# A recommendation tower on one core: the last tiles multiplied without rounding, two items fetched ahead of the second tile's rows

## What is computed

```
e = stack([tbl_f[ids[:, f]] for f in 0..25], axis=1)
z = concat([dense, all products of pairs of (dense, e)])
h = concat([z, dense])
h = maximum(h @ W_top1 + b_top1, 0)      # 607 -> 512
h = maximum(h @ W_top2 + b_top2, 0)      # 512 -> 256
y = h @ W_top3                           # 256 -> 1
```

## Time and profile before

| what | us |
|---|---|
| median of 3 runs | 472.18 (470.95 to 473.91) |
| the profiled execution: its time | 471.37 |
| the profiled execution: its span, first to last instruction | 469.5 |
| POOL busy / PE busy / DVE busy / ACT busy | 396.2 / 417.1 / 338.4 / 223.7 |
| mean granted TensorE clock | 0.967 |

### The profile page before, as it was taken

One profiled execution on the slowest core, in us unless ns is written; L12 is line 12 of the kernel. 1 busy time (PEld: TensorE's weight loads), 2 busy tenths in 40 slices (PEclk: granted clock), 3 DMA queues, 4 the chain that ended last, 5 costly groups with the idle time before them and its releaser, 6 DMA issues.

```text
span 469.5 us, 11728 instructions
## 1 busy us (share of the span) xinstructions
PE 417.1 (89%) x4210; PEld 392.8 (84%) x4210; DVE 338.4 (72%) x777; ACT 223.7 (48%) x727; POOL 396.2 (84%) x553
## 2 busy tenths in 40 slices
PE   0766969989999989998799969999699988999898
PEld 0766869889999979898798969999698978988786
DVE  5897897986888677885597657876678855956260
ACT  3853654536553535455254443545254552536152
POOL 7899999899989998998998998899899899899600
PEclk9988997999999989999899999999899998999999
DMA  7992225122212312231212312222122212121100
GB/s 213 263 227 83 78 80 168 51 75 77 78 44 79 83 39 86 74 82 43 80 45 74 87 40 80 51 77 74 45 82 74 83 43 80 41 80 41 35 2 0
DMA packets 20046, 36.82 MB, mean 78 GB/s; under 512 B 8109, under 2 KB 10677, under 8 KB 19994
## 3 DMA queue, kind: packets, MB, share of 16 engines
q0 software_dynamic: 8704, 17.84, 14.3%
q1 hardware_dynamic: 11290, 18.28, 13.7%
HBM read 36.09 MB, written 0.01 MB: 77 GB/s over the span
## 4 chain that ended last, share of the span: by engine, by line
POOL 55%; issue 28%; PE 6%; DMA 3%; ACT 3%; DVE 2%; SPq 1%; POOLq 1%; DVEq 0%; ACTq 0%
POOL rows L414 29%; POOL y_wide L403 25%; DMA vecs<-in_tbl 3%; PE turn_ps L489 2%; PE dots_ps L473 1%; DVE inter L889 1%; POOLq L402 1%; ACT dots_ps L686 1%; SPq L297 1%; PE turn_ps L554 1%; PE mlp_ps L563 1%; DVE onehot L836 1%; ACT t_hi L679 1%; PE dots_ps L554 1%; DVE t_lo L853 1%
## 5 line engine op out<-in xcount | busy, mean ns | idle before, releaser
L414 POOL DMA_INDIRECT rows<-in_tbl,idx_sb x272 | 261.9, 963 | 45.6 <-POOL y_wide L403 43.7
L836 DVE TENSOR_TENSOR onehot<-ids_sb,late_ps 125x1024 fp32r<-125x1024 int32 (+2 forms) x154 | 167.3, 1143 | 8.2 <-DMA ids_sb<-in_ids_by_round 4.5
L889 DVE COPY_PREDICATED inter<-mask,dots_ps 27x48 f32<-27x48 int32 x496 | 103.1, 208 | 63.0 <-ACT inter L703 44.2
L403 POOL MEMSET y_wide<- 64x448 f32 x272 | 134.2, 493 | 0.2
L703 ACT COPY inter<-dots_ps 27x64 f32<-27x64 f32 x496 | 99.4, 200 | 67.0 <-PE dots_ps L473 54.5
L473 PE MATMUL dots_ps<-vecs 128*64 128x54 f32 x1984 | 117.3, 224 | 1.5 <-ACT vecs L672 0.9
L473 PEld LDWEIGHTS dots_ps<-vecs 128*64 128x64 f32 x1984 | 113.3, 139 | 5.8 <-issue 2.1
L489 PE MATMUL turn_ps<-onehot,t_hi 125*128 125x256 f32 x378 | 103.6, 309 | 13.6 <-DVE vecs L652 10.3
L489 PE MATMUL turn_ps<-onehot,t_lo 125*128 125x256 f32 x378 | 98.3, 295 | 0.0
L489 PEld LDWEIGHTS turn_ps<-onehot,t_hi 125*128 125x128 f32 x378 | 77.5, 205 | 18.5 <-issue 8.5
L489 PEld LDWEIGHTS turn_ps<-onehot,t_lo 125*128 125x128 f32 x378 | 77.5, 205 | 0.2
(11 more groups left out here) (86 smaller groups left out, 371.8 us busy)
## 6 DMA issues: line engine op xcount, KB each, us to landing
ids_sb<-in_ids_by_round SPq DMA_DIRECT2D x25, 384.0 KB
rows<-in_tbl,idx_sb POOLq DMA_INDIRECT x272
vecs<-in_tbl SPq DMA_DIRECT2D x8, 448.0 KB
rows<-in_r_dense_features SPq DMA_DIRECT2D x16, 64.0 KB
h_sb<-in_W_top_laid SPq DMA_DIRECT2D x2, 512.0 KB
vecs<-in_tbl SPq DMA_DIRECT2D x1, 560.0 KB
w_sb<-in_W_top SPq DMA_DIRECT2D x1, 512.0 KB
vecs<-in_tbl SPq DMA_DIRECT2D x8, 52.0 KB
```

The lines of the kernel that those rows point to most:

```text
L403: pool.memset(unread, 0.0).then_inc(pauses_made, 1)
L414: nc.gpsimd.indirect_dma_start(out=rows[v % 2][:, s, :], out_offset=None, in_=tables[f - 1][:, :], in_offset=bass.IndirectOffsetOnAxis(ap= ...
L836: dve.tensor_tensor(part_buffer(k, h)[0:KP, 0:n], home.rearrange("p (o r) -> p o r", o=1).to_broadcast([KP, n, R]), row_of[KT[k]][0:KP, a: ...
L889: dve.copy_predicated(inter_of(u, q, g, a, n), mask[g * 32:g * 32 + N, a:a + n].rearrange("p (j s) -> p j s", s=1).to_broadcast([N, n, QS] ...
```

## The change

**The last step.** `x_hi` and `x_lo` are no longer made for tiles 14 and 15. `end_layer1` multiplies `inter` itself in float32 with `w_hi` and `w_lo` (4 blocks of `inter` and one of `end_dense`, a copy of the dense vectors that ACT makes in `place_dense`): 10 matmuls for each of the 4 parts. Tile 14 is done as a whole (128 columns streamed), its parts 0 and 1 ahead of the transposes of tile 15's fourth row group, parts 2 and 3 ahead of those of the last group. Tile 15 is done unit by unit (64 columns streamed): unit 0 while unit 1's products are still copied and merged, unit 1 at the end. Layers 2 and 3 go by tile too, 128 samples each. The 50 `stay_busy` transposes are gone, layer 3 of the round before has moved forward, and dots of tile 15's second unit wait for ACT's `end_rectify1` of tile 14, which reads the same bank.

**The rounds.** In steps 3 to 6 (of 0 to 7, `soon`) items 3 and 4 are fetched before the last three row groups of the second tile are transposed; `turns`, ACT's copies and DVE's comparisons follow.

```diff
+        FROM = 3
+        def soon(i, r):
+            return i * 2 + r >= FROM
...
+                if n >= FROM:
+                    turns += [("item", n + 1, 3), ("item", n + 1, 4)]
+                turns += [("rows", 2 * n + 1, k) for k in range(2, NG)]
...
+            def end_layer1(i, v, u, bank_of_part, *ms):
+                cols = slice(0, P) if u is None else slice(u * (P // UNITS), (u + 1) * (P // UNITS))
+                units = v * UNITS + (UNITS if u is None else u + 1)
+                pe.wait_ge(inter_by_act, i * (4 * NA) + units * PER_UNIT)
+                pe.wait_ge(inter_by_dve, i * (4 * ND) + units * PER_UNIT)
+                pe.wait_ge(x_hi_made, i * 8 + 4 + v - 1)
+                for m in ms:
+                    for w in (w_hi, w_lo):
+                        for jj in range(JG + 1):
+                            last = pe.matmul(bank_of_part(m)[:, cols], w[:, jj, m * P:(m + 1) * P].bitcast(F32),
+                                             inter[:, jj, cols] if jj < JG else end_dense[:, v - 2, cols],
+                                             start=(w is w_hi and jj == 0), stop=(w is w_lo and jj == JG))
...
+            def end_of_layers(i):
+                end_layer1(i, 3, 0, lambda m: end_ps[m], *range(M1))
+                pe.wait_ge(y_kept, i * 2 + 1)
+                end_layer2(i, 2, end_h2_ps[0])
+                end_layer1(i, 3, 1, lambda m: end_ps[m], *range(M1))
+                end_layer3(i, 2)
+                end_layer2(i, 3, end_h2_ps[1])
+                end_layer3(i, 3)
...
+                if soon(i, r):
+                    fetch(i, r, 3)
+                    fetch(i, r, 4)
                 transpose_rows(i, v + 1, (2, 3, 4))
-                fetch(i, r, 3)
+                if not soon(i, r):
+                    fetch(i, r, 3)
                 dots(i, v + 1, 0)
...
                 layer2(i, 0, 0)
-
-                stay_busy(row_ps, 32)
+                layer2(i, 0, 1)
+                end_layer1(i, 2, None, lambda m: end_first_ps[m], 0, 1)
                 transpose_rows(i, 3, (3,))
-                layer2(i, 0, 1)
-                stay_busy(row_ps, 4)
+                layer3(i, 0)
+                end_layer1(i, 2, None, lambda m: end_first_ps[m], 2, 3)
                 transpose_rows(i, 3, (4,))
                 dots(i, 3, 0)
+                pe.wait_ge(relu1_done, i * (2 * M1) + 2 * M1)
                 dots(i, 3, 1, last_dots_ps)
-                layer3(i, 0)
                 end_of_layers(i)
```

More of the change, by code:

```diff
@@ L250, in dlrm_tower @@
                 turns += [("rows", 1, k) for k in range(2, NG)]
-            turns += [("item", n + 1, k) for k in range(3, X)]
+            turns += [("item", n + 1, k) for k in range(5 if n >= FROM else 3, X)]
         turns += [("rows", 2 * ROUNDS - 2, k) for k in range(NG)] + [("rows", 2 * ROUNDS - 1, k) for k in range(NG)]
@@ L530, in layer3 @@
                 last.then_inc(y_done, 1)
[L532 to L559, removed]
@@ L560, in end_of_layers, with end_layer2 @@
+            def end_layer2(i, v, banks):
+                before = i * (2 * M1) + M1 + (v - 2) * M1
+                mine = slice((v - 2) * P, (v - 1) * P)
+                for ks in (range(M1 - 1), (M1 - 1,)) if v == 3 else (range(M1),):
                     for m in range(M2):
@@ L697, in take_products @@
             def take_products(i, v, u, place=dots_ps):
-                if u == 0 and not (static(i) and i == 0 and v == 0):
+                if u == 0 and i * 4 + v not in (0, 2 * ROUNDS - 1):
                     act.wait_ge(x_lo_made, i * 8 + v * 2)
@@ L717, in split_input, with place_dense, end_rectify1, end_rectify2 @@
                 nc.scalar.copy(x_hi[:, 0:JG, mine], inter[:]).then_inc(x_hi_made, 1)
+            def place_dense(i, v):
+                act.wait_ge(*taken(turn_of["rows", i * 4 + v, 0]))
+                nc.scalar.copy(end_dense[:, v - 2, :].rearrange("p (h two s) -> p h two s", two=2, s=QS),
+                               in_turn(vecs[1][:, v - 2, :, 0])).then_inc(x_hi_made, 1)
+            def end_rectify1(i, v, bank_of_part):
+                mine = slice((v - 2) * P, (v - 1) * P)
+                for m in range(M1):
+                    act.wait_ge(h1_done, i * (2 * M1) + M1 + (M1 if v == 2 else M1 + m + 1))
+                    nc.scalar.activation(end_h1_sb[:, m, mine], bank_of_part(m)[:, 0:P], ACT.Relu,
+                                         bias=b1_sb[:, m:m + 1]).then_inc(relu1_done, 1)
+            def end_rectify2(i, v, banks):
+                mine = slice((v - 2) * P, (v - 1) * P)
+                for m in range(M2):
+                    act.wait_ge(h2_done, i * (2 * M2) + M2 + (M2 if v == 2 else M2 + m + 1))
+                    nc.scalar.activation(end_h2_sb[:, m, mine], banks[m], ACT.Relu,
+                                         bias=b2_sb[:, m:m + 1]).then_inc(relu2_done, 1)
             def rectify1(i, r, *ms):
@@ L798, in last_step @@
                 take_vectors(i, 3, 1)
+                place_dense(i, 2)
                 rectify1(i, 0, 3)
-                split_input(i, 2)
-                act.wait_ge(*taken(turn_of["rows", i * 4 + 3, 0]))
-                split_dense(i, 3)
+                rectify2(i, 0, 0, 1)
                 take_vectors(i, 3, 3)
-                rectify2(i, 0, 0, 1)
+                place_dense(i, 3)
+                end_rectify1(i, 2, lambda m: end_first_ps[m])
                 take_products(i, 3, 0)
                 take_products(i, 3, 1, last_dots_ps)
[L808 to L815, removed]
+                end_rectify2(i, 2, end_h2_ps[0])
+                end_rectify1(i, 3, lambda m: end_ps[m])
+                end_rectify2(i, 3, end_h2_ps[1])
             written_out(step, last_step)
```

58 lines of the change are left out of this document (33 added, 25 removed).

## The result

The changed kernel takes 484.63 us (median of 4 runs, 483.73 to 486.17), beside 471.56 us for the kernel before in the same session (4 runs, 470.27 to 473.91). The ratio is 1.0275, with a 95% interval of 1.0223 to 1.0326: slower by 13.1 us. The forecast was 484.7.

What follows compares the result with a forecast made beforehand. POOL's gathers bound the kernel until the last is issued at 441.39 us, then PE's work before and the chain behind the last rows. 471.37 us plus 13.3, with 0 for the moved fetches, gave 484.7; range 480.5 to 488.

Steps and rivals of the forecast that it cites:

- In front of the last rows (1): PE's work before tile 15's last rows: tile 14's parts and layer 3 delay tile 15's dots by 5.05 us.
- ACT, copies, merges (2, 3): Last step: ACT's rectifying of tile 14 costs nothing; copies and merges keep their pace, unit 1 merged at 460.99.
- Behind unit 0 (4): PE after unit 0's merge: each unit takes 9.12 us, layer 2 of tile 14 1.87; PE is late, ending 479.7.
- Cheap units (0.12): Rival on tile 15's units: 64-column records cost 0.068 us, units 5.44 us each, time 477.3; chance 0.12.
- Everything by the column (0.04): Rival on layer 1: float32 records priced by columns streamed, at twice the pace; time 465.0, faster; chance 0.04.
- The clock: Rival: PE idles, gets clock 0.50 in the last step; one stretch 486.4, two 488; second stretch or late PE 0.08.
- The moved fetches (6): Rounds 4 to 7: some 5 us of PE per round gained, returning as waits for rows; effect on time 0.

Runs made afterwards that it cites:

- half of tile 14's layer: Changed kernel with tile 14's first layer from `w_hi` alone, the `w_lo` products left out: 479.36 us (1 run).
- the split matmuls: Changed kernel with each layer 1 matmul of tile 15's two units split into two of 64 loaded columns, output halves alternating, same sums: 475.91 us (1 run).
- the hybrid: Kernel before, rounded operands kept, only tile 14's layer 1 moved in front in place of filling transposes, layers 2 and 3 by tile: 469.22 us, ratio 0.9968.

## Why the prediction was right, step by step

| step of the prediction | predicted | measured |
|---|---|---|
| record 128 loaded, 128 streamed | 0.117 us | 0.112 and 0.114 (40 in 4.47 and in 4.57, start to start) |
| record 128 loaded, 64 streamed | 0.114 us | 0.1117 (40 in 4.47) |
| a unit of tile 15 | 9.12 us | 9.08 and 8.88 |
| delay of tile 15's dots | 5.05 us | 4.59 (449.58 less 444.99) |
| layer 2 of tile 14 | 1.87 us | 1.84 |
| from the dots' start to the end of the span | 32.8 us | 32.4 |
| moved fetches | 0 | 0.3 (ratio 1.0007, interval -0.2 to +0.9 us) |
| more than before, in all | 13.3 us | 12.5 in the span, 13.1 in the medians |

**In front of the last rows (1).** Right. The delay is 0.46 us smaller than said. The records give 0.32 of it: tile 14's 80 took 9.04 us (438.12 to 442.59, 444.07 to 448.64), not 9.36. PE also came to the third row group 0.25 us sooner, at 434.04, and the pieces between took 0.11 more. The run with half of tile 14's layer shows that this stretch counts in full.

**ACT, copies, merges (2, 3).** Right. Unit 1 was merged at 460.26 (predicted 460.99; 0.46 of the difference is the dots' own), 7.3 us before PE came to it at 467.58.

**Behind unit 0 (4).** The step that decided, and right: the two kinds of record cost the same, since one pass of 128 columns takes 9.17 us and a unit of 64 takes 9.08 or 8.88. Cheap units (0.12) fell with that. The reason I gave held within its bounds only. "Each hidden under the matmul before it but not under another load" fits where neighbours load the same columns, as nearly everywhere in the rows that I had; the split matmuls show it wrong as a general rule, and so do the pairs from 448.42 on in the kernel before. The change loads all 128 columns each time, so the price came out right all the same.

The loads of 128 columns in the changed kernel last 192 ns and those of 1 column 82, a difference of 110. The Trainium skill's rule of columns divided by 1.2 GHz ("TensorE: Matmul & The Clock Gate", section "LDWEIGHTS (loading the stationary operand)") gives an estimate of 107, and the trace agrees.

**Everything by the column (0.04).** It didn't come. Its point of decision, a 128 by 128 record under some 0.07 us, was missed by 0.04.

**The clock.** The two slow stretches feared in the last step didn't come; the clock is 1.00 from 430 to 480 us. The condition under which they were feared, an idle PE ahead of tile 14's last rows, came only in part: it waited 0.85 us there. With the moved fetches alone it waited 2.41 us, and the slow stretch came, at no cost.

**The moved fetches (6).** The effect on the time, 0, was right, and so was the way: what PE gains ends in waits for tile 14's rows (at 416.46 here, said for 416.6) and tile 15's third group (1.42 us instead of 0.92). The picture beside it failed. "The second tile's rows no longer wait 2.5 us in rounds 4 to 7, and the slow stretches there are gone or elsewhere": they still wait 2.57, 2.19 and 2.03 us in rounds 5 to 7, and the slow stretch stands where it stood, longer in that profile; only in round 4 is it gone. The sum's own argument, that POOL doesn't wait for PE and whatever PE gains comes back as a wait for rows, should have told me that the wait in the same round comes back too, since its rows come at a time that POOL sets.

**The number.** That the median lies 0.07 us from the forecast is luck. The parts added up 0.8 us too high (a span of 482.8 for 482.0), and the median happened to lie 0.9 above the time of the profiled execution (483.73), for which they were added up.

## What to carry to other kernels

Count weight loads before cutting a matmul into passes: with 128 columns loaded and 128 or 64 streamed, a record cost 0.112 us here, so a second pass over the same weights costs as much as the first, and it pays only if it hides more than that. Where few columns are streamed (64 here, float32), split the loads by output halves and alternate them; the same sums then took half the time. No run splits matmuls of 128 streamed columns, or rounded ones. And when a busy engine becomes faster, look at its clock behind the new waits before you believe the gain.

## What the runs showed of the hardware that I had not expected

- **Loads of different halves run beside each other.** With 64 columns loaded and 64 streamed, float32, a record costs 0.0575 us beside neighbours of its own output half, and 0.030 when halves alternate (80 in 2.33 to 2.48 us). The dots (64 loaded, 54 streamed) go from 3.7 us a unit to 1.9. The Trainium skill says on "TensorE: Matmul & The Clock Gate", section "The mechanism", that a load overlaps matmuls in flight only when the row group differs. Here all records use the same 128 rows and only the columns differ, and they overlap: the measurement decides.
- **From 128 columns down, a record is not cheaper for streaming less.** 128 or 64 columns streamed, float32 or rounded operands (24 in 2.68 us in the hybrid): 0.112 us in each case, with 128 columns loaded. With 256 streamed in float32 it is 0.216.
- **A slow stretch costs what stands in it.** The same wait of about 2 to 2.5 us in round 7 was followed by 3.40 us at a clock of 0.50 in the kernel before and by 6.80 us at 0.51 in the changed one. In mid-program this was free. In the last step, 2.06 us of waits in two pieces brought on 3.4 us at 0.52 and put 1.3 us on the end.
